# Ten zeroing transfers issued together behind the index lists, and the norm's shift placed ahead of the next clamp, in a one-core graph layer

## The reference, cut to what matters

```python
h = x @ W_in2f                                   # 6250 x 128
Wij = ssp(f_ij @ W_filt1 + b_filt1) @ W_filt2 + b_filt2
Wij = Wij * edge_weight[:, None]
x_ij = h[dst] * Wij
agg = segment_sum(x_ij, src, num_segments=6250)
out = ssp(agg @ W_out1 + b_out1) @ W_out2 + b_out2   # ssp = softplus - log 2
return layernorm(x + out)                        # over the 128 columns
```

## Time and profile before

| | |
|---|---|
| median of three runs | 2242.66 us (2235.79 to 2242.95) |
| the profiled execution | 2232.01 us, span 2230.1 us from the first to the last instruction |
| busy in the span | PE 2044.0, DVE 1889.0, POOL 1747.9, ACT 1591.8 us |
| head, up to the first matmul of the middle (L1768) | 110.04 us |
| zeroing transfers | 20 of 640 KB, ACT's queue |

### The profile page before, as it was taken

The page is one execution under the profiler, slowest core; times in us unless marked ns, Lnnn a source line. Parts: engine busy times, 40 slices in busy tenths (PEclk is TensorE's granted clock), DMA queues, the critical chain, the costliest instruction groups (busy, mean ns, idle before and its releaser), DMA issues.

```text
span 2230.1 us, 54072 instructions
## 1 busy us (share of the span) xinstructions
PE 2044.0 (92%) x15953; PEld 1681.7 (75%) x15953; DVE 1889.0 (85%) x3919; ACT 1591.8 (71%) x3812; POOL 1747.9 (78%) x1078
## 2 busy tenths in 40 slices
PE   3479999999999999999999999999999999999945
PEld 2357878787878778877878887788878787878733
DVE  6468989898989889988989898898989898989836
ACT  0278777777777777877778777777777777778616
POOL 2048888888888888888888888888888888888873
PEclk9589999999999999999999999999999999999978
DMA  6746666666666665656666656656666666666494
GB/s 234 279 85 104 94 94 96 101 101 88 99 99 89 98 98 94 95 90 106 98 90 100 95 93 100 99 94 94 97 100 97 91 100 96 92 97 96 55 234 128
DMA packets 353785, 239.34 MB, mean 107 GB/s; under 512 B 86919, under 2 KB 332786, under 8 KB 353338
## 3 DMA queue, kind: packets, MB, share of 16 engines
q0 software_dynamic: 146736, 66.85, 32.2%
q1 hardware_dynamic: 196326, 152.61, 27.1%
q10 hardware_dynamic: 10476, 16.77, 2.0%
HBM read 147.25 MB, written 88.83 MB: 106 GB/s over the span
## 4 chain that ended last, share of the span: by engine, by line
DMA 35%; PE 23%; POOL 16%; issue 15%; DVE 5%; ACT 3%; POOLq 0%; ACTq 0%; DVEq 0%; SPq 0%
DMA table<-total,index 33%; POOL table L716 16%; PE unit_psum L1824 6%; PE unit_psum L1843 4%; PE both_psum L1781 4%; PE total_psum L1794 3%; PE pre_psum L1768 2%; PE both_psum L1806 1%; PE both_psum L1777 1%; DMA h_parts<-h_out 1%; DMA b_o<-in_b_o 1%; ACT out_rows L1082 1%; ACT total L852 1%; DVE scat_hot L1377 1%; DVE route_hot L1360 1%
## 5 line engine op out<-in xcount | busy, mean ns | idle before, releaser
L716 POOL DMA_INDIRECT table<-total,index x1019 | 1689.2, 1658 | 428.9 <-issue 255.5
L1824 PE MATMUL unit_psum<-moving,route_hot 128*128 128x258 f32 x3808 | 602.7, 297 | 9.1 <-ACT ring L893 5.8
L1824 PEld LDWEIGHTS unit_psum<-moving,route_hot 128*128 128x128 f32 x3808 | 496.2, 191 | 72.3 <-ACT ring L893 51.4
L893 ACT ACTIVATE ring<-unit_psum 128x258 fp32r<-128x258 f32 x952 | 353.4, 394 | 245.6 <-PE unit_psum L1824 227.2
L869 ACT ACTIVATE h_dst<-both_psum,cols 128x128 f32<-128x128 f32 x1564 | 445.0, 373 | 96.5 <-PE both_psum L1806 95.1
L1843 PE MATMUL unit_psum<-scat_hot,ring 64*128 64x448 f32 x3808 | 461.1, 379 | 10.5 <-DVE scat_hot L1377 6.3
L1377 DVE TENSOR_SCALAR scat_hot<-node_iota,ring 128x448 fp32r<-128x448 uint16 x952 | 433.0, 474 | 9.1 <-ACT ring L893 5.0
L1781 PEld LDWEIGHTS both_psum<-w_f,hidden 128*128 128x128 f32 x3128 | 423.7, 196 | 11.6
L1781 PE MATMUL both_psum<-w_f,hidden 128*128 128x128 f32 x3128 | 421.6, 278 | 0.0
L1360 DVE TENSOR_SCALAR route_hot<-node_iota,cols 128x896 fp32r<-128x896 uint16 x544 | 378.9, 715 | 45.2 <-PE unit_psum L1824 44.2
L1843 PEld LDWEIGHTS unit_psum<-scat_hot,ring 64*128 64x128 f32 x3808 | 340.1, 185 | 89.3 <-ACT ring L893 30.3
(11 more groups left out here) (118 smaller groups left out, 1507.4 us busy)
## 6 DMA issues: line engine op xcount, KB each, us to landing
dst_b<-dst SPq DMA_DIRECT2D x391, 128.0 KB
src_b<-src SPq DMA_DIRECT2D x255, 128.0 KB, 3.4
f_t<-in_f_t SPq DMA_DIRECT2D x100, 256.0 KB, 3.6
table<-total,index POOLq DMA_INDIRECT x1019
table<-zeros ACTq DMA_DIRECT2D x20, 640.0 KB, 5.6
window<-h_parts SPq DMA_DIRECT2D x391, 32.0 KB
parts<-table SPq DMA_DIRECT2D x48, 256.0 KB, 5.0
h_parts<-h_out SPq DMA_DIRECT2D x12, 384.0 KB, 5.4
```

The source lines that it names most:

```text
L716: pool.indirect_dma_start(tables[table], bass.IndirectOffsetOnAxis(index[:, i, k:k + 1], 0), total[:, i, k, 0:DIM], None, compute_op=ALU.a ...
L893: act.activation(ring[:, r[1] % RING, k, :], unit_psum[:, k % 2, 0:MOVING], ACT.Copy).then_inc(ring_done, 1)
L1824: last = pe.matmul(unit_psum[:, k % 2, 0:MOVING], route_hot[:, tile, k * P:(k + 1) * P], moving[:, tile, :], start=(tile == 0), stop=(tile ...
```

## The change

In the head, the loop's even chunks no longer issue their two transfers for tables 1 and 3. These ten go out one behind the other after ACT's work on chunk 1, behind a wait for both stored index lists. Table 2's transfer in the odd chunks and table 0's stay. In the tail, DVE's shift of chunk i-2 moves to the front of step i, ahead of the clamp of chunk i. Nothing is added to or taken from what is computed or moved.

```diff
@@ split_h (ACT)
                 if not isinstance(c[0], int):
-                    for k in range(1 + b, TABLES, 2):
-                        zero(k, c[0])
+                    if b == 1:
+                        zero(2, c[0])
                 else:
                     zero(0, min(2 + c[1], FIFTHS - 1))
                 act.wait_ge(h_mm, after_chunk(c))
...
                 act.activation(h_out[:, b, 0:tiles, 1, :], h_rest[:, b, 0:tiles, :], ACT.Copy).then_inc(h_mid, 1)
+                if is_at(c, 1):
+                    act.wait_ge(edges16_stored, 32)
+                    for fifth in range(FIFTHS):
+                        zero(1, fifth)
+                        zero(3, fifth)
@@ last_layers (DVE)
             def last_layers(i):
+                c = plus(i, -2)
+                if is_chunk(c):
+                    b, tiles = c[1] % 2, tiles_of(c)
+                    dve.wait_ge(e_inv, after_chunk(c))
+                    previous(dve, e_norm, c, after_chunk)
+                    dve.scalar_tensor_tensor(norm_shift[:, b, 0:tiles], mean_var[:, b, 0:tiles, 0], -1.0,
+                                             inv_dev[:, b, 0:tiles], ALU.mult, ALU.mult).then_inc(e_shift, 1)
+
                 c = i
                 if is_chunk(c):
...
                     dve.tensor_scalar(soft[:, b, 0:n], pre_psum[:, b, 0:n], b_o1[:, 0:1], EXP_ARG_MAX,
                                       ALU.add, ALU.min).then_inc(e_clamp, 1)
-
-                c = plus(i, -2)
-                if is_chunk(c):
-                    b, tiles = c[1] % 2, tiles_of(c)
-                    dve.wait_ge(e_inv, after_chunk(c))
-                    previous(dve, e_norm, c, after_chunk)
-                    dve.scalar_tensor_tensor(norm_shift[:, b, 0:tiles], mean_var[:, b, 0:tiles, 0], -1.0,
-                                             inv_dev[:, b, 0:tiles], ALU.mult, ALU.mult).then_inc(e_shift, 1)
```

## The result

| | before | after |
|---|---|---|
| median of five runs each (of before, the three shown above and two more) | 2239.19 us (2235.79 to 2242.95) | 2226.66 us (2221.04 to 2230.55) |
| ratio, 95% interval | | 0.9939, 0.9922 to 0.9957 |
| the profiled execution (its span) | 2232.01 us (2230.1) | 2227.48 us (2225.5) |
| first matmul of the middle (L1768, now L1773) | 110.04 us | 100.53 us |
| from there to the first `agg_t` of the tail | 2043.7 us | 2051.1 us |

What follows compares the result with a forecast made beforehand. The head's loop was taken as bound by DMA bytes, the tail by a ring of waits, with the middle unchanged. Gains of 9.3 (head) and 5.9 (tail) sum to 15.2 us, from the median 2242.66 to 2227 us; range 2213 to 2238.

Steps and rivals of the forecast that it cites:

- The step from row to turn: Head loop: a 2.96 us chain of work plus a 3.0 us store landing makes a 5.96 us turn; four turns save 9.3 us.
- The row at 71.45: Head: a store of `h_parts` that landed in 2.85 us, one zeroing transfer issued 1.46 us before; basis for the 3.0 landing.
- Two issues in 1.28 us: Head, ACT's queue: the measure from which ten early issues were forecast to take about 6.4 us, from some 29 to 36.
- Rival 4: Head: ACT is held at its ten issues and comes late to L794 of chunk 2; 2251 us at 6 us each; 5%.
- The term: Tail: moving the shift ahead of the clamp shortens nine periods by 5.3 us and the first shift by 0.6, 5.9 together.
- while POOL still adds tables the shift takes 0.36 in place of 0.15: Tail: the longer shift makes the ring on DVE and ACT 4.59 us in five early periods.
- the ring on DVE and ACT: Tail: waits from `hidden` through shift, `out_rows`, `agg_t` and Exp to the next `hidden`; forecast 4.38 us, 0.67 less than 5.05.
- PE's ring: Tail: waits from `agg_t` through `hidden`, L2065 and the transposes to the next `agg_t`; forecast to set the period at 4.45 us.
- Rival 1: Head: store and remaining zeroing transfer share the wire evenly; landing some 4 us, turn 7.0, head wins 5.2, time 2231.6; 15%.
- Rival 2: Tail: the ring closes elsewhere (PE's transposes, POOL's sums or statistics), period stays near 5.05; only head's 9.3 counts, 2233.4 us; 11%.
- Rival 3: Middle: it gives the head's gain back, leaving the tail's 5.9 us; 2236.8 us, not to be told from no change; 13%.
- my own last sign of being wrong: Middle: the prediction was to count as wrong if the middle grew by what the head lost.

## Why the prediction was right, and where it was not

**The head.** The step from row to turn held. I took 3.0 us for the landing and 5.96 for a turn; 3.13 on the chain (median of all 2.8) and 6.1 came out. Four turns give 33.18 - 24.40 = 8.8 us; from L794 of chunk 2 to the first matmul of the middle it is 44.26 - 35.89 = 8.4, and this length stays within 0.3 us over all runs with the same number of transfers in a turn (44.1 to 44.3 with three, 35.8 to 36.1 with one). So 8.4 of the forecast 9.3 belong to the change. The remaining 1.1 of the measured 9.5 are luck: L794 of chunk 2 came earlier by that much, but L794 of chunk 0 had already come 0.98 us earlier (23.14 against 24.12), ahead of the first moved transfer. That the ten transfers drain by 56 to 61 us held nearly as well: just after 55.

Two readings in that part were loose. The row at 71.45 was said to have one zeroing transfer for company; two more went out in the middle of its landing, so it was no bare pairing:

```profile
72.36 0.85 ACTq L773 DMA_DIRECT2D table<-zeros  x2
```

And 8.7 us for the bytes of a turn that took 8.3 cannot be right: in the four turns the wire moved 393 GB/s, the 377 are a mean over 70 to 110 us, with the beginning and the end of the loop in it.

**The issues of ACT.** Two issues in 1.28 us were no safe measure for ten: 12.09 us, 1.2 each, against my 6.4. Over the six executions with ten early issues it was 5.38 to 12.09. Nothing came of it, as ACT is free at 41.5 and asked for at 64.64. Rival 4 begins to cost at 37 us for the ten.

**The tail.** The term was mis-sized: 5.9 us forecast, 2.5 in the trace (2.5 in the nine periods of the part alone too; 5.6 with 2.0 to 9.0 by its times). The step that failed is "while POOL still adds tables the shift takes 0.36 in place of 0.15". I took 0.36 from the earlier trace rows as a duration. The same trace has, for POOL:

```profile
2177.38 1.28 POOL L760 TENSOR_TENSOR half_sum<-half_sum,parts 128x512 f32<-128x512 f32 x1
```

This addition ends at 2178.66, and the shift at 2178.31 + 0.36 = 2178.67: the 0.36 was the rest of a wait. Moved ahead of the clamp, the shift meets the additions earlier and waits up to 1 us more, so six periods stay between 4.93 and 5.28 us. The periods after POOL has finished are 4.28, shorter than my 4.45: the ring on DVE and ACT sets them (0.66 + 0.19 + 1.55 + 1.88). PE's ring, the 4.45, was too long by its last steps: 1.72 + 0.06 from L2065 to `agg_t`, of which the 0.06 stands in no row; in the changed kernel 1.60 us pass there (2201.11 to 2202.71).

The Trainium skill (SBUF — State Buffer, "Who interferes with whom") says that VectorE and GpSimd share one pair of ports under an exclusive lock, that a VectorE instruction with two inputs in SBUF contends with a GpSimd instruction that reads SBUF, and that one with at most one input in SBUF does not contend outside its 2-port modes. The same page ("SBUF: two separate sides") says that whoever starts first gets the pair for the whole instruction. The runs agree where POOL is first: the waits end within 0.02 us of POOL's instruction, and 0.15 us is left with one operand in PSUM. That POOL waits when the shift is first is not shown.

**The rivals.** Rival 1, even sharing, would have given turns near 7; those are of two transfers, not one. The landing by it was 4 us, and 3.1 were measured on the chain; so the rule of the Trainium skill that stood beside this rival (DMA: Bandwidth & Descriptors, "Queues, rings and completion order": each DMA engine goes round the queues that have work, packet by packet) was not enough to size a landing here. Rival 2 was half right in its effect, since the early periods did not shorten, but not through PE's transposes. Rival 3 had the measure of the noise: the middle took 2043.7 to 2057.0 us over the twelve profiled executions, more than either part is worth, and before happened to have the shortest. That it gives back the head's gain is not borne out: the head alone is 11.0 us (7.4 to 14.8) faster. By my own last sign of being wrong, a middle that grows by what the head lost, the one profiled execution (7.4 of 9.5) would have misled. Why the middle varies stays open; PE's busy time in it is no answer, with 1959.7 us in one of the two longest and 1964.8 in one of the shortest.

**The sum.** 15.2 against 13.7 (9.6 to 17.5). By the traces the change itself is worth 8.4 + 2.5 = 10.9 us, which the interval holds too; that 13.7 lies so near 15.2 is in part luck. That 2227 was met within 0.4 us owes something to the scale, since the median of before is 2239.19 with two more runs and not 2242.66; the difference is the fair measure. The timed interval is too wide to show the 3.4 us that the tail lacks; only the trace does.

## What to carry to other kernels

Where one stretch is short of bytes and its neighbour leaves the wire empty, move bytes, count megabytes before and behind, and stop when the chain has passed from transfers to a ring of waits. Before a short instruction is moved, look at whose instruction ends when it ends: a duration can hold a wait, and the new place may have a longer one. The two remedies belong together: the reordering gave 2.45 us of the nine periods (46.05 to 43.60), and one operand moved from SBUF to PSUM another 4.8 (to 38.79). Moved in the old order, which was not run, the operand could have saved little, as no shift of before waited more than 0.22 us. And compare the granted clock of two tails before their lengths.

## What the runs showed of the hardware

- A DVE instruction on 128x4 elements that takes 0.15 us alone took up to 1.17 beside a POOL addition, and the trace books all of it as busy time. With one of its two tensors in PSUM it took 0.15 or 0.16 in all thirteen chunks.
- Ten issues of 640 KB on ACT's queue took 5.38, 6.57, 6.63, 7.62, 11.27 and 12.09 us in six executions; fifteen took 14.12, 16.11 and 18.23. The two long ones of ten are those whose chunk 0 came early (L794 at 23.14 and 23.39 us, against 23.89 to 24.30). What sets this was not settled.
- TensorE's granted clock fell from 1.00 to 0.50 near the end of the tail (from 2214 us on in the changed kernel), and the eight products of L2074 then took 1.92 us, where they had taken 1.06.
- The landing of a 384 KB store went 5.3, 3.7, 2.8, 2.6 us with 3, 2, 1 and 0 zeroing transfers in a turn: most of the gain is in the first two taken out.
